# Recommender tower on one core: the first table's ids by a broadcast DMA, and one subtraction per table

## The reference

```python
e = jnp.stack([tbl_0[ids[:, 0]], ..., tbl_26[ids[:, 26]]], axis=1)   # 512 x 27 x 128
dot_products = jnp.einsum('bnd,bmd->bnm', e, e)
r, c = np.tril_indices(27, k=-1)
z = dot_products[:, c, r]                                            # 512 x 351
h = jnp.concatenate([z, dense_ctx], axis=1)                          # 512 x 367
h = jnp.maximum(h @ W_top1 + b_top1, 0.0)                            # 512 x 512
h = jnp.maximum(h @ W_top2 + b_top2, 0.0)                            # 512 x 256
y = h @ W_top3                                                       # 512 x 1
```

## Time and profile before

| | us |
|---|---|
| median of 3 runs | 109.08 |
| lowest, highest run | 108.71, 110.86 |
| span of the profiled execution | 123.6 |
| TensorE busy in it | 106.3 (86%) |
| VectorE busy | 70.0 (57%) |
| ScalarE busy | 67.2 (54%) |
| GpSimd busy | 68.1 (55%) |

### The profile page before, as it was taken

How to read it: one execution, slowest core, us unless ns; L and a number is a source line. 1 busy time by engine, 2 the same in 40 slices (tenths; PEclk the granted TensorE clock), 3 DMA queues, 4 the chain that set the end, 5 groups by cost and what they waited for, 6 DMA issues and landing times.

```text
span 123.6 us, 3473 instructions
## 1 busy us (share of the span) xinstructions
PE 106.3 (86%) x1496; PEld 86.1 (70%) x1496; DVE 70.0 (57%) x98; ACT 67.2 (54%) x112; POOL 68.1 (55%) x71
## 2 busy tenths in 40 slices
PE   6998799899999899999329993789458999997992
PEld 6534487687887687788219883669448999797891
DVE  6799999999999999999900050015001060103401
ACT  4596929899999999995200052025301144531442
POOL 3777888888888888887744166416560665000000
PEclk9999999999999999999985599558975699999999
DMA  3896366966984574711210101110200011000000
GB/s 79 262 237 190 101 204 146 293 198 155 302 235 111 172 229 108 205 48 42 54 52 17 31 29 42 27 48 21 66 24 27 21 48 41 23 5 5 5 0 1
DMA packets 5305, 12.06 MB, mean 98 GB/s; under 512 B 1765, under 2 KB 2277, under 8 KB 5290
## 3 DMA queue, kind: packets, MB, share of 16 engines
q1 hardware_dynamic: 3282, 7.75, 22.0%
q0 software_dynamic: 1984, 4.07, 12.8%
q10 hardware_dynamic: 24, 0.02, 0.1%
HBM read 11.83 MB, written 0.00 MB: 96 GB/s over the span
## 4 chain that ended last, share of the span: by engine, by line
PE 68%; DVE 16%; issue 13%; ACT 1%; DVEq 0%
PE ring L512 21%; PE gram_ps L539 12%; DVE marks L651 10%; PE gram_ps L512 8%; PE ring L592 5%; PE ids_ps L574 4%; PE ring L523 4%; DVE low L628 3%; PE ids_ps L567 2%; PE ids_ps L523 2%; PE ring L574 2%; PE ring L602 2%; PE ids_ps L592 1%; DVE pick L610 1%; PE ids_ps L553 1%
## 5 line engine op out<-in xcount | busy, mean ns | idle before, releaser
L422 POOL DMA_INDIRECT rows<-tbl,ids_sb x62 | 67.1, 1082 | 36.3 <-issue 15.9
L651 DVE TENSOR_TENSOR marks<-ids_ps,row_no 125x1024 fp32r<-125x1024 f32 (+2 forms) x39 | 43.5, 1148 | 0.0
L512 PE MATMUL ring<-marks,high 125*128 125x512 f32 (+1 forms) x64 | 26.6, 416 | 1.7 <-issue 1.6
L539 PE MATMUL gram_ps<-rowsT 128*27 128x27 f32 x1024 | 15.8, 206 | 11.4 <-issue 11.2
L512 PE MATMUL ring<-marks,low 125*128 125x512 f32 (+1 forms) x64 | 25.2, 394 | 0.0
L539 PEld LDWEIGHTS gram_ps<-rowsT 128*27 128x27 f32 x1024 | 13.3, 118 | 14.7 <-issue 14.0
L512 PEld LDWEIGHTS ring<-marks,high 125*128 125x128 f32 x64 | 12.8, 200 | 7.1 <-issue 4.6
L724 ACT ACTIVATE away<-ids_ps,row_no 125x512 f32<-125x512 f32 (+1 forms) x22 | 14.0, 715 | 4.7 <-PE ids_ps L466 4.1
L628 DVE TENSOR_TENSOR low<-raw,high 125x512 fp32r<-125x512 f32 (+1 forms) x23 | 16.2, 705 | 0.0
L672 DVE STREAM_TRANSPOSE gram<-gram_ps 128x416 f32<-128x416 f32 (+1 forms) x8 | 4.6, 612 | 18.1 <-PE gram_ps L539 18.1
L512 PEld LDWEIGHTS ring<-marks,low 125*128 125x128 f32 x64 | 12.9, 202 | 1.6
(11 more groups left out here) (61 smaller groups left out, 116.5 us busy)
## 6 DMA issues: line engine op xcount, KB each, us to landing
raw<-tbl SPq DMA_DIRECT2D x9, 448.0 KB
raw<-tbl SPq DMA_DIRECT2D x2, 560.0 KB
rows<-tbl,ids_sb POOLq DMA_INDIRECT x62
w_sb<-w SPq DMA_DIRECT2D x2, 256.0 KB
w_sb<-w SPq DMA_DIRECT2D x1, 512.0 KB
raw<-tbl SPq DMA_DIRECT2D x9, 52.0 KB
raw<-tbl SPq DMA_DIRECT2D x2, 224.0 KB
w_sb<-w SPq DMA_DIRECT2D x1, 192.0 KB
```

What stands on the lines that cost most here:

```text
L422: nc.gpsimd.indirect_dma_start(out=rows[0:n, i % ROW_BUFS, s, :], out_offset=None, in_=tables[PLACES[s]], in_offset=bass.IndirectOffsetOnA ...
L512: last = nc.tensor.matmul(bank[:, 0:n], part[:, i % SPLIT_BUFS, c * D:(c + 1) * D], mark_of(unit, c), start=c == 0 and part is high, stop= ...
L539: last = nc.tensor.matmul(gram_ps[s * STRIP:s * STRIP + F, g, 0:F], places, places, start=True, stop=True)
L651: nc.vector.tensor_tensor(marks_of(unit)[:, c0 - c1:, :], index.to_broadcast([TP, c1 - c0, n]), which.to_broadcast([TP, c1 - c0, n]), ALU. ...
```

## The change

- A new DMA ahead of the `fids` DMA on ScalarE's queue copies the first row of `found_ids` (2 KB) to all 128 partitions of `first_ids` (int32).
- VectorE makes the marks of job 0 from `first_ids` in SBUF, chunk by chunk: eight `tensor_scalar` operations of 125 x 512 in place of one 512-wide, one 512-wide and three 1024-wide `tensor_tensor` operations on `ids_ps`. It waits for that DMA and not for TensorE.
- The cast of `fids` moves on VectorE from ahead of the row numbers to behind job 0's first unit. TensorE's three `spread_ids` before the first step are now for jobs 1, 2 and 3, and still stand ahead of `find 0 0`.
- `pick` is one 128 x 12 copy. The matmul reads a column of it with a step of zero. The second copy of nine columns is gone.
- `subtract` takes a whole table (1024 or 1280 numbers a partition) and stands behind the job's first unit. For job 0 it takes the second half, as before. `low_ready` counts tables.
- On ScalarE `split(1)` moves ahead of the first `mark`.

```diff
 def lows(j):
-    return 2 * j + 1
+    return j + 1
...
-        pick = sb("pick", [P, len(FOUND), P], F32R)
+        pick = sb("pick", [P, len(FOUND)], F32R)
+        first_ids = sb("first_ids", [P, B], I32)
...
             def spread_ids(j):
                 b0, n = JOBS[j]
-                if j >= IDS_BANKS:
+                if j - IDS_BANKS >= 1:
                     pe.wait_ge(marked, through(BY_DVE, j - IDS_BANKS))
-                if j - IDS_BANKS >= 1:
                     pe.wait_ge(away_ready, j - IDS_BANKS)
-                if j == IDS_BANKS:
-                    pe.wait_ge(pick_ready, 2)
-                nc.tensor.matmul(ids_ps[:, j % IDS_BANKS, 0:n], pick[:, j, :], fids_r[:, b0:b0 + n],
+                nc.tensor.matmul(ids_ps[:, j % IDS_BANKS, 0:n], pick[:, j:j + 1].to_broadcast([P, P]), fids_r[:, b0:b0 + n],
                                  start=True, stop=True).then_inc(spread, 1)
...
-            for j in range(IDS_BANKS):
+            for j in range(1, IDS_BANKS + 1):
                 spread_ids(j)
...
-                        pe.wait_ge(low_ready, lows(i) - 1 + half)
+                        pe.wait_ge(low_ready, lows(i))
...
-            pick_for(0, IDS_BANKS)
-            dve.wait_ge(fids_cleared, 1)
-            dve.wait_ge(fids_in, 16)
-            nc.vector.tensor_copy(fids_r[0:len(FOUND), :], fids[:, :]).then_inc(fids_ready, 1)
+            nc.vector.tensor_copy(pick[:, :], ident[:, 0:len(FOUND)]).then_inc(pick_ready, 1)
...
-            def subtract(j, h):
+            def ids_ready():
+                dve.wait_ge(fids_cleared, 1)
+                dve.wait_ge(fids_in, 16)
+                nc.vector.tensor_copy(fids_r[0:len(FOUND), :], fids[:, :]).then_inc(fids_ready, 1)
+
+            def subtract(j):
                 dve.wait_ge(high_ready, j + 1)
-                d0, d1 = (x * D for x in chunks_in(j, h))
+                d0, d1 = (HALF[0] if j == 0 else 0) * D, CHUNKS[j] * D
...
-                if c0 == 0:
-                    dve.wait_ge(spread, j + 1)
-                    if j >= 1:
-                        dve.wait_ge(away_ready, j)
+                if u == 0:
+                    dve.wait_ge(first_ids_in, 16)
+                elif c0 == 0:
+                    dve.wait_ge(spread, j)
+                    dve.wait_ge(away_ready, j)
...
+                if j == 0:
+                    for c in range(c0, c1):
+                        last = nc.vector.tensor_scalar(mark_of(unit, c), first_ids[0:TP, 0:n],
+                                                       row_no[CHUNKS[j]][0:TP, c:c + 1], None, ALU.is_equal)
+                        if c == 0:
+                            last.then_inc(first_marked, 1)
+                    last.then_inc(marked, 1)
+                    if c0 == HALF[0]:
+                        subtract(0)
+                    if u == 0:
+                        ids_ready()
+                    return
...
-                if c0 in (0, HALF[j]) and (j, c0) != (0, 0):
-                    subtract(j, int(c0 != 0))
-                if u == 1:
-                    pick_for(IDS_BANKS, len(FOUND))
+                if c0 == 0:
+                    subtract(j)
...
+            nc.scalar.dma_start(first_ids[:, :], found_ids[0:1, :].to_broadcast([P, B])).then_inc(first_ids_in, 16)
             nc.scalar.dma_start(fids[:, :], found_ids).then_inc(fids_in, 16)
...
-                act.wait_ge(spread, j + 1)
+                act.wait_ge(spread, j)
...
+            split(1)
             mark(BY_ACT[0])
```

More of the change, by code:

```diff
@@ L282, in build @@
         fids_in = sem("fids_in")
+        first_ids_in = sem("first_ids_in")
         first_half_in = [sem(f"first_half_in{h}") for h in range(2)]
@@ L492, in _ @@
                     else:
-                        pe.wait_ge(low_ready, lows(i) - 1 + half)
+                        pe.wait_ge(low_ready, lows(i))
                     for unit in units_in(i, half):
                         _, c0, c1 = unit
-                        if c1 == CHUNKS[i] and i + IDS_BANKS < len(JOBS):
+                        if c1 == CHUNKS[i] and i >= 1 and i + IDS_BANKS < len(JOBS):
                             spread_ids(i + IDS_BANKS)
@@ L607, in _ @@
         def _(dve):
-            def pick_for(j0, j1):
-                nc.vector.tensor_copy(pick[:, j0:j1, :], ident[:, j0:j1].rearrange("p (k o) -> p k o", o=1)
-                                      .to_broadcast([P, j1 - j0, P])).then_inc(pick_ready, 1)
             nc.vector.memset(gram_ps[:, :, :], 0.0).then_inc(gram_cleared, 1)
@@ L750, in _ @@
                 for unit in units:
-                    if unit[1] == 0 and unit[0] + 1 < SPLIT_BUFS:
+                    if unit[1] == 0 and 2 <= unit[0] + 1 < SPLIT_BUFS:
                         split(unit[0] + 1)
```

## The result

| | before | after |
|---|---|---|
| median us | 109.05 (6 runs) | 114.82 (6 runs) |
| lowest, highest | 108.71, 110.86 | 113.99, 115.72 |
| ratio | | 1.0505, 95% interval 1.0455 to 1.0555 |
| span of the profiled execution | 123.6 | 112.7 |

The change makes the kernel 5% slower; 106.5 us had been forecast. The span of the first profile of before can't be compared: it is 14.5 us above its own plain runs. Up to 58.7 us the two profiles of before agree within 0.1 us, so the earlier trace rows of that stretch stand.

What follows compares the result with a forecast made beforehand. VectorE was taken to pace the kernel to about 57 us, TensorE close behind. Gains of 1.9 us by job 2 and 0.6 over jobs 2 to 10, together 2.5, came off the median 109.08: 106.5 us, range 105.4 to 109.2.

Steps and rivals of the forecast that it cites:

- What bounds the kernel: Whole kernel: VectorE paces it to about 57 us, TensorE 0.2 us a job behind; time saved there moves the rest forward.
- The DMA that pushes others back: Start: the 256 KB for `first_ids` push the other early loads back by 1.0 us, covered for the tables.
- The landing of `first_ids`: Start of job 0: it lands and the first mark starts at 3.7 us, bounds 2.8 and 4.7.
- The marks at 0.33: VectorE, job 0: each new mark takes 0.33 us like the cast, eight cost 2.64 instead of 4.60.
- The wait for ScalarE: VectorE ahead of job 0's subtraction: an idle wait of about 1.5 us takes part of the marks' gain.
- VectorE's gain at job 2: Job 2's first mark on VectorE starts at 13.3 instead of 15.27 us, a gain of 1.9.
- The subtraction: VectorE, later jobs: one whole subtraction of 1.13 replaces halves of 1.20; period 4.53, 0.6 us over jobs 2 to 10.
- The step of zero: TensorE's load of a `pick` column: took 0.19 us, a change in it priced at zero, at most 2.3.
- TensorE's first matmuls: TensorE, job 0: start at 4.8, spreads 1.3, eight plain float32 matmuls 3.5, ending at 9.6 us.
- The rival that priced half a clock at this place: TensorE, rested ahead of the spreads, gets half its clock; eight matmuls cost 3.5 more; 109.1 us, chance 0.15 shared with GpSimd coming last.
- The rival of the lock: Shared ports: VectorE's eight marks and the cast each wait for a GpSimd gather, 4.3 us slower, 113.4 us; chance 0.08.
- The rival that named GpSimd: GpSimd hardly rests and could come last, its first gathers starting no earlier; no gain, 109.1 us, chance 0.15 shared with half clock.

Runs made afterwards that it cites:

- the swapped order: The changed kernel with ScalarE's two DMAs in the other order, `fids` first and the broadcast into `first_ids` behind it: 110.28 us, ratio 1.006 to the kernel before.
- the second profile of before: The kernel before, unchanged, profiled once more: span 107.8 us, its run at 109.64 us.

## Why the prediction was wrong, point by point

Between 106.5 and 114.8 us lie 8.3 us: 2.5 that were forecast as a gain and did not come, and 5.8 of loss. The steps that failed are the landing of `first_ids` for the first part, and for the second the harm to `ids_sb`, which the prediction put at nothing.

- **What bounds the kernel.** Right for the kernel before up to 58.7 us. What failed stands in the last sentence: that what VectorE gives back moves the rest forward unchanged. In the run with the small `pick` alone 1.4 us were given back and 1.0 arrived. In the last turn of tile 2 the last row of GpSimd's stream comes 1.7 us before it is needed. I had read the gathers as off the chain and not asked how late they may be. The rows were at hand: gaps of 0.30 before every gather mean a stream that can't catch up, and its end is first start + 1.25 a gather + what VectorE holds it up.
- **The DMA that pushes others back.** I went through the first table's halves and tables 1 and 2, and left out `ids_sb`, a small transfer of 31 KB, for which GpSimd waits before it can start a stream that has no rest. It landed 4.8 us after its issue and not 1.9. This alone starts the gathers 2.9 us late, and the swapped order, which undoes it, gave 4.5 of the 5.8 us back.
- **The landing of `first_ids`.** 3.7 forecast, 2.8 to 4.7 as bounds, 5.42 measured. The term that was missing is the repeated row, 1.3 us (4.4 against 3.1 to landing; 4.7 in the changed kernel); the prediction had it only as a remark in a rival.
- **The marks at 0.33.** 0.40 measured, nearer to the cast than to the mark from PSUM; 0.6 us over eight.
- **The wait for ScalarE.** 1.5 forecast, 1.17 measured. The mechanism was right.
- **VectorE's gain at job 2.** 1.9 forecast, -0.1 measured: 1.8 from the late start (5.52, not 3.7), 0.6 from the marks, less the 0.3 of the shorter wait.
- **The subtraction.** Period 17.68 - 13.15 = 4.53 as forecast, but of the 0.6 us that it was to bring over jobs 2 to 10, 0.1 arrived in the run with it alone. That VectorE's period sets TensorE's, one of the signs that the prediction named, does not hold any more once the period is shorter: TensorE, which was put 0.2 us a job behind, then paces itself.
- **The step of zero.** Priced at nothing, and 188 ns a load both ways.
- **TensorE's first matmuls.** Forecast was a start at 4.8, then 1.3 for the spreads and 3.5 for the plain float32 matmuls, 9.6 in all. Measured are 6.78 for the start, 1.45 and 4.6: 12.8. The 1.1 us on the matmuls are those at half speed. The rival that priced half a clock at this place had 3.5 for it; that the rest is the cause is not shown. A fall behind a wait in tile 2 no rival had. The finds still end only 0.1 us later than before, so all of this is made up by 58.7 us.
- **The rival of the lock.** One pair of ports, as the Trainium skill has it (SBUF — State Buffer, section "SBUF: two separate sides"): the traces agree that GpSimd is shut out while VectorE makes its marks, 2.58 for a gather of 0.95 otherwise. They do not agree that whoever starts first keeps the pair: a mark that started inside a gather lost at most 0.14 us. I had priced only this reverse direction, as 113.4 with a chance of 0.08, and the direction that holds at nothing. It costs the stream 1.3 us (2.58 against 1.24). That the time came out near 113.4 is chance; the mechanism was another.
- **The rival that named GpSimd** as the last to come had the right engine, at 109.1 and 0.15. It let the stream start as before, so it ended at no gain instead of a loss.

Lateness of gather 47: 2.9 us from the start, 1.3 from the first gather, some 0.8 from longer holds of later gathers, 0.6 of it by gather 8: 5.0 in all. Its row lands 2.6 us behind it and not 2.7, and 1.7 us are the slack; 5.0 - 0.1 - 1.7 = 3.2, and the third transpose of the turn comes at 76.3 instead of 73.1.

**Open** is what makes the holes of 0.7 to 1.7 us in TensorE's work, most of them near 69 to 73 and 77 to 84 us. The traces hold one lead: in every profile but the first of before, a transfer of 16 KB in the DMA queue of instructions ends near the start of such a hole, between 0.7 us ahead of it and 0.4 us behind (68.82 to 70.13 in the second profile of before, whose hole starts at 70.32). But most such transfers have no hole behind them, and in the first profile of before the holes at 59 to 63 us have none near, so the cause is not shown. Open, too, is why the clock falls behind the hole in one kernel and not in another.

## What to carry to other kernels

A transfer that is added at the start is priced by what it stands ahead of, down to the smallest one: ask of every load issued in the same instant who reads it and how much slack that reader has. An engine that is never on the chain of waits but also never rests is a deadline; work out when its last item comes, and compare with when it is taken. A wait inserted in front of TensorE can cost its own length and then half speed behind it.

## What was not expected of the hardware

- 128 reads of one 2 KB row of HBM landed after 4.4 us, 128 reads of different rows after 3.1, each in the same place at the start.
- Two DMAs issued in the same instant from two queues: the one of 31 KB landed with the one of 256 KB (4.8 and 4.7 us). Issued 0.65 us ahead it took 1.9.
- A gather beside back-to-back `tensor_scalar` marks ends 0.12 to 0.13 us behind the last of them (2.58 and 2.37 us instead of 0.94); it gets in between none of them. A mark that starts inside a gather loses 0.14 us at most.
- In the changed kernel the weight loads of TensorE's plain float32 matmuls stepped by 0.85 us up to 11.5 us and by 0.43 from there on, while the profile's clock column read 1.00.
- A hole of 1.46 us in TensorE's stream stood ahead of matmuls that wait for nothing.
